# A recommender tower on one core: eight folded slices in place of four on GpSimd, and two pair tiles made a slice earlier

## What is computed

```python
def _cin_layer(X0, Xi, W, b):
    Wr = W.reshape(H, F0, Fi)
    return jnp.einsum('hjk,bjd,bkd->bhd', Wr, X0, Xi) + b[None, :, None]

e = stack([tbl_f[ids[:, f]] for f in range(39)], axis=1)      # 1024 x 39 x 16
Xi = e
for W, b in ((W0, b0), (W1, b1), (W2, b2)):                   # H = 128
    Xi = _cin_layer(e, Xi, W, b)
    res.append(Xi.sum(axis=2))
h = concatenate([concatenate(res, axis=1), dense_ctx], axis=1)
h = maximum(h @ W_top1 + b_top1, 0.0)
h = maximum(h @ W_top2 + b_top2, 0.0)
y = h @ W_top3
```

## Time and profile before

| | us |
|---|---|
| median of 3 runs (1355.66 to 1356.35) | 1356.19 |
| the profiled execution's own time | 1354.27 |
| span of the profile, first to last instruction | 1352.5 |
| PE busy | 1273.0 |
| DVE, ACT, POOL busy | 1061.5, 1052.3, 957.1 |

### The profile page before, as it was taken

One profiled execution on the slowest core, in us unless ns is written; L12 is line 12 of the kernel. 1 busy time (PEld: TensorE's weight loads), 2 busy tenths in 40 slices (PEclk: granted clock), 3 DMA queues, 4 the chain that ended last, 5 costly groups with the idle time before them and its releaser, 6 DMA issues.

```text
span 1352.5 us, 20729 instructions
## 1 busy us (share of the span) xinstructions
PE 1273.0 (94%) x6069; PEld 1039.2 (77%) x6069; DVE 1061.5 (78%) x2683; ACT 1052.3 (78%) x3352; POOL 957.1 (71%) x693
## 2 busy tenths in 40 slices
PE   3279999999999999999999999999999999999998
PEld 3257677787878888788877878788887888778877
DVE  4158888978798778977889778977789777987895
ACT  2248888887888878887888878887788878887784
POOL 6778888867887778867888777877788455564201
PEclk7579999999999999999999999999999999999999
DMA  6252412132222412232222322214122221220000
GB/s 227 35 120 60 74 46 70 45 51 55 54 50 57 74 31 54 62 51 55 55 60 46 60 49 51 60 46 74 45 53 49 49 60 50 53 53 15 1 2 0
DMA packets 68522, 74.38 MB, mean 55 GB/s; under 512 B 47363, under 2 KB 52996, under 8 KB 68282
## 3 DMA queue, kind: packets, MB, share of 16 engines
q1 hardware_dynamic: 58426, 70.49, 22.4%
q0 software_dynamic: 9984, 2.58, 2.2%
HBM read 12.64 MB, written 2.56 MB: 11 GB/s over the span
## 4 chain that ended last, share of the span: by engine, by line
PE 80%; DVE 7%; issue 5%; ACT 3%; POOL 2%; SPq 2%; DMA 1%; DVEq 0%; ACTq 0%; POOLq 0%
PE ring L1082 19%; PE ring L1084 18%; PE ring L1083 18%; PE side L969 5%; PE side L1004 4%; PE l_ps L955 4%; PE l_ps L956 3%; PE l_ps L957 3%; DVE x_r L827 3%; DVE terms L871 2%; ACT terms L658 2%; PE side L1033 1%; PE side L1042 1%; SPq L343 1%; POOL e_in L406 1%
## 5 line engine op out<-in xcount | busy, mean ns | idle before, releaser
L658 ACT ACTIVATE terms<-ring,xb 128x128 f32<-128x128 f32 x2944 | 844.2, 404 | 210.1 <-PE ring L1084 197.1
L871 DVE SCALAR_TENSOR_TENSOR terms<-ring,xb,terms 128x128 f32<-128x128 f32 x1792 | 507.8, 344 | 96.7 <-PE ring L1084 94.2
L1082 PE MATMUL ring<-w_hi,x_hi 128*128 128x512 f32 (+1 forms) x1280 | 556.2, 435 | 11.1 <-DVE terms L871 5.9
L1084 PE MATMUL ring<-w_hi,x_lo 128*128 128x512 f32 (+1 forms) x1280 | 497.9, 389 | 0.0
L1083 PE MATMUL ring<-w_lo,x_hi 128*128 128x512 f32 (+1 forms) x1280 | 497.2, 388 | 0.0
L827 DVE TENSOR_REDUCE x_r<-terms 128x32 f32<-128x800 f32 (+1 forms) x512 | 463.5, 927 | 0.1
L450 POOL TENSOR_TENSOR pairs_lo<-pairs,pairs_hi 117x1024 fp32r<-117x1024 f32 (+1 forms) x104 | 250.4, 2408 | 174.9 <-ACT pairs_hi L553 174.4
L406 POOL DMA_INDIRECT e_in<-in_tbl,idx x312 | 306.5, 982 | 76.3 <-issue 69.4
L1082 PEld LDWEIGHTS ring<-w_hi,x_hi 128*128 128x128 f32 x1280 | 241.7, 189 | 74.6 <-DVE terms L871 14.7
L1084 PEld LDWEIGHTS ring<-w_hi,x_lo 128*128 128x128 f32 x1280 | 240.8, 188 | 52.3
L1083 PEld LDWEIGHTS ring<-w_lo,x_hi 128*128 128x128 f32 x1280 | 242.7, 190 | 43.6
(11 more groups left out here) (114 smaller groups left out, 692.7 us busy)
## 6 DMA issues: line engine op xcount, KB each, us to landing
pairs<-x_both SPq DMA_DIRECT2D x303, 156.0 KB
x_rep<-x_both SPq DMA_DIRECT2D x45, 156.0 KB
e_in<-in_tbl,idx POOLq DMA_INDIRECT x312
terms<-in_L_rec_W SPq DMA_DIRECT2D x1, 2496.0 KB, 11.2
x_scratch<-e_df SPq DMA_DIRECT2D x8, 312.0 KB, 9.2
xb<-x_scratch SPq DMA_DIRECT2D x8, 312.0 KB, 5.2
g_t<-in_L_rec_W SPq DMA_DIRECT2D x4, 512.0 KB, 6.0
g_t<-x_both SPq DMA_DIRECT2D x8, 156.0 KB
```

The source lines that it names most:

```text
L658: last = nc.scalar.activation(term(d, ACT_BEFORE[d][g] + i), twos(ring[:, (GROUPS * d + g) % RING, i * H:(i + 1) * H]), ACT.Copy, scale=sc ...
L871: nc.vector.scalar_tensor_tensor(out=acc, in0=y, scalar=scale_of(j, d, odd), in1=acc, op0=ALU.mult, op1=ALU.add).then_inc(dve_unit, 1)
L1082: nc.tensor.matmul(acc, x1_hi[:, x], w1_hi[:, w], start=True, stop=False)
L1084: nc.tensor.matmul(acc, x1_lo[:, x], w1_hi[:, w], start=False, stop=True).then_inc(y_group, 1)
```

## The change

`FOLDED` grows from four slices to eight: 0, 5, 8 and 13 are folded too. In a chunk (not in the first filling of the pipeline) tile 0 is made in slice 6 instead of slice 7, and tile 7 in slice 14 instead of slice 15; slices 7 and 15 make none. In these two slices GpSimd multiplies behind the blocks instead of at the slice's start. Since ScalarE and GpSimd ask the same `tile_made`, the rounding of tile 0 moves to (6, 7) and that of tile 7 to (14, 7), and the subtractions to the ends of slices 6 and 14. TensorE uses the tiles where it did. SP issues the read-back of the scales behind tile 5's copy instead of behind tile 0's.

```diff
-    FOLDED, FOLD = (6, 7, 14, 15), 6
+    FOLDED, FOLD = (0, 5, 6, 7, 8, 13, 14, 15), 6
...
     FIRST_MADE = 7
+    LATE_MADE = (6, 14)
 
     def tile_made(c, d, layer1, following):
 
-        if d < PAIR_TILES - 1:
-            return (c, PAIR_TILES + 1 + d) if layer1 else None
-        if d == D - 1:
-            return (c + 1, PAIR_TILES) if following else None
-        if not FIRST_MADE <= d < FIRST_MADE + PAIR_TILES:
-            return None
-        return (c + 1, d - FIRST_MADE) if following else None
+        if d < PAIR_TILES - 1 and layer1:
+            return (c, PAIR_TILES + 1 + d)
+        if layer1:
+            made = {6: 0, 14: PAIR_TILES}.get(d, d - FIRST_MADE if FIRST_MADE < d < D - 1 else None)
+        elif d == D - 1:
+            made = PAIR_TILES
+        else:
+            made = d - FIRST_MADE if FIRST_MADE <= d < FIRST_MADE + PAIR_TILES else None
+        return (c + 1, made) if following and made is not None else None
...
                         pair_tile(c + 1, i, 1 - odd)
-                        if i == (0 if layer1 else FROM_PE + 1):
+                        if i == (0 if layer1 else PAIR_TILES - 2):
                             xb_back()
...
-                    if made:
+                    if made and d not in LATE_MADE:
                         multiply_pairs(*made)
...
                             make_block(c - 1, r, 1 - odd)
+                    if made and d in LATE_MADE:
+                        multiply_pairs(*made)
                     if layer1 and d in FOLDED:
                         pool.wait_ge(act_group, scaled(c, d, FOLD_GROUP))
```

## The result

| | before | after |
|---|---|---|
| median of 4 runs, us | 1355.93 (1354.07 to 1356.35) | 1372.42 (1371.69 to 1373.15) |
| span of the profile, us | 1352.5 | 1369.8 |

The ratio is 1.0129 (95% interval 1.0117 to 1.0141; the two medians alone give 1.0122): slower by 16.5 us in the medians, where the prediction had 19.3.

What follows compares the result with a forecast made beforehand. TensorE was taken to bound the kernel. Five chunks at 1.9 + 0.7 us (13.0) plus 6.3 in chunk 0 gave 19.3, on 1356.2 a median of 1375.5 us; own range 1366 to 1383, wider 1362 to 1385.

Steps and rivals of the forecast that it cites:

- What bounds the kernel: TensorE, busy 94% of the span, has no slack: any new wait is paid in full; relieving VectorE counts as nothing.
- Slice 6, chunks 1 to 5: GpSimd makes tile 0 late, ScalarE's rounding waits 2.0 us, the pooling matmul at (6, 9) starts 1.9 us later.
- Slice 14: Chunks 1 to 5: tile 7's late rounding delays group 7's scalings for (15, 1); 0.7 us lost, bounds nothing and 1.3.
- Chunk 0: Late GpSimd costs 1.6 us at slice 0's fold, 4.0 for slices 5 and 6, 0.7 in slice 14: together 6.3.
- Chunks 6 and 7: Chunk 6 has few gathers left, chunk 7 makes no tile for a next chunk: no loss.
- The read-back: SP issues it behind tile 5's copies, about slice 11; nothing waits for it there: no cost.
- The range: Sums of bounds gave 1369 to 1383 us; the forecast's own range 1366 to 1383, the wider one 1362 to 1385.
- Nothing changes: Rival: GpSimd comes in time after all, or ScalarE's wait falls into time lost anyway; 1356 us, chance 0.10.
- Faster: Rival: GpSimd comes in time and TensorE's waits for VectorE go; 1338.6 us at most, 1350 nearer, chance 0.07.
- Much slower by VectorE: Rival: GpSimd's new folds each hold VectorE up for 1.89 us, net 35 us; about 1410 us, chance 0.03.

Runs made afterwards that it cites:

- the relief alone: Kernel before, VectorE's sums of slices 0, 5, 8 and 13 leaving out six terms that GpSimd does not add either: 1354.89 us, ratio 1.0002.
- the read-back alone: Kernel before with only the read-back's condition changed, which moves it in the first filling of the pipeline alone: 1355.39 us, ratio 1.0002.
- e5: Changed kernel with ScalarE's rounding of tiles 0 and 7 moved from group 7 to group 9 of slices 6 and 14: 1358.49 us, ratio 1.0027.
- e2: Kernel before with tile 0 made in slice 6 and tile 7 in slice 14, without the four more folds: 1357.17 us, ratio 1.0019.
- e4: Changed kernel without the folds of slices 5 and 13; tiles' new places and read-back stay: 1359.51 us, ratio 1.0029.
- e9: Changed kernel with tiles 0 and 7 rounded at group 9 and the first two pooling evacuations moved to (6, 7) and (7, 1): 1349.34 us, ratio 0.9955.
- e10: Changed kernel without the fold of slice 13 alone: 1369.86 us, ratio 1.0111.
- e1: Kernel before with only the four more folds (slices 0, 5, 8, 13), tiles 0 and 7 staying in slices 7 and 15: 1362.32 us, ratio 1.0060.
- e8: Changed kernel with the first two pooling products' evacuations moved to (6, 7), ahead of the rounding, and (7, 1): 1354.83 us, ratio 0.9998.

## Why the prediction came out as it did

**What bounds the kernel.** Right. TensorE has no slack, so each stop was paid; a relief of VectorE by 25 us is worth nothing, as the relief alone shows.

**Slice 6, chunks 1 to 5.** The mechanism was right, the term too large: 1.9 us a chunk predicted, 1.73 in even chunks (11.51 in place of 9.78) and 1.33 in odd ones (11.11). The even chunk, the kind that I had read, fits step by step: from GpSimd's tie to the end of the multiplication 798.74 - 778.65 = 20.1 us (predicted 20.24), ScalarE's wait 1.94 (2.0), rounding and scalings 800.78 - 798.82 = 1.96 (1.96). Row lengths overlap by a few hundredths, which I had added up as if they did not. For the odd chunks I had read nothing: there the tie comes earlier. GpSimd and ScalarE in chunk 3, which begins at 570.21:

```profile
619.65 2.40 POOL L453 TENSOR_TENSOR pairs_lo<-pairs,pairs_hi 117x1024 fp32r<-117x1024 f32 x1 [4.16 <-ACT pairs_hi L558]
```

```profile
639.84 1.06 ACT L558 ACTIVATE pairs_hi<-pairs 117x1024 fp32r<-117x1024 f32 x1 [1.51 <-POOL pairs L442]
```

The tie lies 49.44 us into chunk 3 and 49.86 into chunk 4; the wait is shorter by just that 0.4, and so is the loss. This is where most of the 2.8 us between 19.3 and 16.5 comes from: in five chunks slice 6 gave 2 x 1.73 + 3 x 1.33 = 7.5, not 9.5. With 3.2 from slice 14 (predicted 3.5) and 5.9 from chunk 0 (6.3) the predicted terms measure 16.6.

**Slice 14.** 0.61 to 0.65 measured for 0.7: right, and neither bound was near. Tile 7's copies were not late.

**Chunk 0.** 6.3 predicted. Its stops on TensorE, and behind the second of them the next two matmuls:

```profile
113.36 0.50 PE L960 MATMUL l_ps<-pairs_hi,v_hi 117*128 117x512 f32 x1 [1.49 <-POOL pairs_lo L453]
...
162.39 0.60 PE L960 MATMUL l_ps<-pairs_hi,v_hi 78*128 78x512 f32 x1 [2.07 <-POOL pairs_lo L453]
162.78 0.63 PE L961 MATMUL l_ps<-pairs_hi,v_lo 78*128 78x512 f32 x1
163.21 0.63 PE L962 MATMUL l_ps<-pairs_lo,v_hi 78*128 78x512 f32 x1
...
171.08 0.78 PE L974 MATMUL side<-blocks,x_r 128*128 128x320 f32 x2 [0.93 <-ACT g_t L564]
```

Slice 1 grew by 1.76 (predicted 1.6), slice 6 by 3.82 (4.0), slice 15 by 0.61 (0.7), slice 8 gave back 0.33: 5.9. The remaining 1.1 of the chunk's 7.0 is nearly all the later start of this execution (first scaling at 101.67 in place of 100.68), which the read-back alone did not reproduce.

In slice 6 the predicted path held: tile 0's multiplication ended 11.2 us into the slice (11.4 predicted), and the pooling matmul waited last for the evacuation behind the rounding. But the sum lacked something, and that it didn't show is luck. Behind the stop of 2.07 us TensorE's granted clock was 0.50 from 162.7 to 166.0 (1.2 GHz in place of 2.4), and matmuls followed each other after 0.43 us in place of 0.23. The two waits grew by 1.78 and 0.51, the slice by 3.82: the other 1.5 us are the slow matmuls. They lie ahead of the wait for the evacuation, which would have been that much longer without them (argued from the rows, not tried). In e5, where nothing waits there for the rounding, they are paid: a stop of 2.10, the clock at 0.50 from 162.5 to 165.8, and a slice of 13.72. In the folds alone the same stop of 2.10 was followed by a clock of 1.00 and a slice of 12.18.

One reason was misread: I gave the first gathers for GpSimd's late start, but its first multiplication there, that of tile 8, waits last for the tile's copy, 1.28 us before and 5.92 in the changed kernel.

**Chunks 6 and 7.** Right: 156.61 in both kernels.

**The read-back.** Priced right and read wrong. I wrote, in the section on the change too, that it goes behind tile 5's copy in the chunks. The condition gives 0 for layer 1 in both kernels, so in a chunk it stays behind tile 0's copies; only the first filling changes. SP's queue after the change, chunk 4:

```profile
785.89 4.34 SPq L346 DMA_DIRECT2D pairs<-x_both  x3
790.35 0.48 SPq L369 DMA_DIRECT2D xb<-x_scratch  x1
792.65 62.74 SPq L346 DMA_DIRECT2D pairs<-x_both  x17
```

**The range.** Two of its bounds do not follow from the sums beside them: the high side counts chunk 0 with 8.3, where its own bound is 7 (that gives 25.5 and 1382), and the forecast's own range begins at 1366, where the sum gives 1369. The measurement lies well inside either way.

**The rivals.** "Nothing changes" would have needed room before the tie; the idle time of 4.16 us ahead of it is unchanged and the stretch behind it has none. "Faster" fell with the relief alone. "Much slower by VectorE": with 64 folds beside them the sums take 768 to 985 ns, as with 32. The shared read port of which the Trainium skill warns (Perfetto Trace Analysis, Optimizing Scalar/DVE Operations) shows no effect on them here. Moving the work between the two did not help, as that section warns that it might not, but the runs give another cause.

## What to carry to other kernels

Before giving an engine with idle time more work, go through its list from the last instruction at which it is tied to another engine to the next one that another engine waits for; idle time ahead of the tie can't be used behind it. A wait costs what stands behind it in the waiting engine's list: moving ScalarE's rounding behind the evacuation took back 13 of 16.5 us (by the two spans 11 of 17) with all the work still in place, and moving two evacuations ahead of unrelated work gained 0.8% in a kernel whose busiest engine was at 94%. And read more than one turn of the loop: alternate chunks differed by a fifth of the loss.

## What the runs showed of the hardware that I had not expected

**A new stop of TensorE costs some 0.27 us more than the wait that the trace shows.** Waits of 0.34, 0.41, 0.56 and 1.49 us that were not there before lengthened their slices by 0.61, 0.69, 0.83 and 1.76; taking a wait of 0.42 away shortened slices 6 and 7 by 0.67 and 0.64. Where a wait only grew, from 0.42 to 2.16, the slice grew by the same 1.73. So a stop that is new costs more than its row, and one that only grows costs its growth. The three rows of the second stop above show where the difference comes from. Without a stop a matmul follows the one before after 0.23 us, while that one's row is 0.40 long; the wait is counted from the row's end, so 0.17 of lost overlap is not in it. And the first matmul behind the stop is followed after 0.34 instead of 0.23 or 0.24. Together 0.34 + 0.17 + 0.10 = 0.61, as measured.

**Behind a stop of two microseconds TensorE's clock was often halved.** In slice 6 of chunk 0, stops of 2.06 to 2.50 us were followed by a granted clock of 0.50 in the profiled executions of the changed kernel, e2, e4, e5, e9 and e10, but not in those of e1 and e8 (2.10 in both). In chunk 4 a stop of 2.16 was followed by 1.00 in the changed kernel, one of 2.17 by 0.50 in e10. What decides between them is not shown. Where nothing covered it, this cost 1.2 us (e10, chunk 4) and 1.5 (e5 against e1, chunk 0), about as much as all of the loss in slice 6 of an odd chunk (1.33).

**The same copy holds ScalarE up longer in even chunks.** The copy that ScalarE makes at (4, 5) lasts 1.03 to 1.04 us in either kind of chunk, and the scalings ahead of it start equally late in both (45.45 and 45.47 us into the chunk). Chunk 4, then chunk 3:

```profile
774.24 1.16 ACT L663 ACTIVATE terms<-ring,xb 128x128 f32<-128x128 f32 x4 [1.54 <-PE ring L1089]
775.42 1.03 ACT L576 ACTIVATE x_both<-side 58x512 f32<-58x512 f32 x1
776.48 1.16 ACT L663 ACTIVATE terms<-ring,xb 128x128 f32<-128x128 f32 x4
```

```profile
615.68 1.15 ACT L663 ACTIVATE terms<-ring,xb 128x128 f32<-128x128 f32 x4 [1.82 <-PE ring L1089]
616.70 1.04 ACT L576 ACTIVATE x_both<-side 58x512 f32<-58x512 f32 x1
617.52 1.11 ACT L663 ACTIVATE terms<-ring,xb 128x128 f32<-128x128 f32 x4
```

The starts follow each other after 1.18 and 1.06 us in chunk 4, after 1.02 and 0.82 in chunk 3: 0.40 together, the difference of the ties. In chunk 3 the instructions overlap by some 0.1 to 0.2 us, in chunk 4 they don't. The same two patterns stand at all four of these copies in chunks 1 to 6 of both kernels. Why was not tried and stays open; the chunks copy into different halves of their buffer in turn.
